# The depthwise convolution of an attention layer: its taps on VectorE, in the second pass of each group of heads

## What is computed

```python
qkvo = einsum('oc,bchw->bohw', qkvo_w, x) + qkvo_b          # q, k, v and a gate o
lepe = conv_general_dilated(v_ch, lepe_w, padding='SAME', feature_group_count=C)   # 5x5, one filter a channel
y    = softmax(q k^T * SCALE) v  + lepe + lepe_b            # 12 heads of 32 channels
x    = x + proj(y * o)
```

## Time and profile before

| what | value |
|---|---|
| median of 3 launches | 11554.08 us (11551.97 to 11557.6) |
| profiled launch, and its span from first to last instruction | 11558.28 us, 11556.5 us |
| TensorE busy | 9370.7 us, 81% |
| VectorE busy | 7579.1 us, 66% |
| ScalarE, GpSimd busy | 4167.8 us, 36%; 3974.5 us, 34% |
| mean granted TensorE clock | 0.84 of full |
| chain that ended last | PE 63%, DVE 20%, ACT 6%, issue 6% |

### The profile page before, as it was taken

How to read it: one execution, slowest core, us unless ns; L and a number is a source line. 1 busy time by engine, 2 the same in 40 slices (tenths; PEclk the granted TensorE clock), 3 DMA queues, 4 the chain that set the end, 5 groups by cost and what they waited for, 6 DMA issues and landing times.

```text
span 11556.5 us, 104310 instructions
## 1 busy us (share of the span) xinstructions
PE 9370.7 (81%) x37272; PEld 4302.3 (37%) x37272; DVE 7579.1 (66%) x5637; ACT 4167.8 (36%) x4762; POOL 3974.5 (34%) x1678
## 2 busy tenths in 40 slices
PE   6985888688986889778896798868898688977656
PEld 2223333443334433344333433344333443334433
DVE  3127666866768566776668666686666866677892
ACT  1114334333333333432344333433334333343441
POOL 0004333432334323443334323343233433343560
PEclk8666888788987989889897898879898798988778
DMA  1002111421114211232113311142111421123231
GB/s 33 4 19 91 48 48 55 128 80 51 50 67 122 71 41 58 86 99 71 48 56 107 92 52 52 57 125 75 52 48 71 119 73 46 50 99 93 85 107 46
DMA packets 423038, 802.30 MB, mean 69 GB/s; under 512 B 226128, under 2 KB 241872, under 8 KB 422352
## 3 DMA queue, kind: packets, MB, share of 16 engines
q1 hardware_dynamic: 422480, 795.13, 21.4%
HBM read 698.28 MB, written 71.04 MB: 67 GB/s over the span
## 4 chain that ended last, share of the span: by engine, by line
PE 63%; DVE 20%; issue 6%; ACT 6%; DMA 2%; DVEq 1%; SPq 1%; ACTq 1%; POOL 0%; POOLq 0%
PE ps L910 10%; DVE R L1654 9%; PE ps L883 8%; PE ps L992 7%; PE ps L863 7%; PE ps L756 7%; PE ps L989 5%; DVE ps L1644 4%; PE ps L894 4%; PE ps L1077 3%; ACT R L1182 3%; PE ps L1060 2%; PE ps L975 2%; DVE nmx L1583 1%; PE ps L965 1%
## 5 line engine op out<-in xcount | busy, mean ns | idle before, releaser
L1368 POOL TENSOR_TENSOR R<-R 128x1024 f32<-128x1024 f32 x1536 | 3678.4, 2396 | 5539.3 <-DVE ps L1644 5512.5
L1654 DVE TENSOR_TENSOR_SCAN R<-R,ps 128x1024 f32<-128x1024 f32 x1536 | 3506.7, 2283 | 537.9 <-ACT R L1242 441.4
L1242 ACT ACTIVATE R<-R,negA 128x1024 f32<-128x1024 f32 x1536 | 1753.8, 1144 | 2773.7 <-DVE R L1654 2515.9
L1644 DVE TENSOR_TENSOR ps<-R 128x1024 f32<-128x1024 f32 x1536 | 1997.1, 1300 | 65.5 <-DVE R L1654 7.0
L992 PEld LDWEIGHTS ps<-ident,R 128*128 128x128 f32 x12288 | 1611.2, 159 | 1115.9 <-issue 789.1
L992 PE MATMUL ps<-ident,R 128*128 128x128 f32 x12288 | 1839.0, 304 | 215.3 <-POOL R L1368 163.5
L1583 DVE TENSOR_REDUCE nmx<-ps 128x2 f32<-128x1024 f32 x768 | 936.2, 1219 | 963.4 <-PE ps L863 958.9
L989 PE MATMUL ps<-R,ident 128*128 128x512 f32 x1440 | 946.1, 792 | 433.9 <-ACT R L1232 430.6
L1182 ACT ACTIVATE R<-ps 128x1024 f32<-128x1024 f32 x768 | 786.1, 1024 | 1324.7 <-PE ps L883 1324.3
L910 PE MATMUL ps<-R 128*128 128x512 f32 x2400 | 1245.0, 642 | 0.0
L883 PE MATMUL ps<-R 33*128 33x512 f32 x3072 | 1017.8, 745 | 160.0 <-ACT R L1182 70.0
(11 more groups left out here) (154 smaller groups left out, 6151.8 us busy)
## 6 DMA issues: line engine op xcount, KB each, us to landing
R<-bc_scratch SPq DMA_DIRECT2D x1024, 512.0 KB, 3.8
R<-in_x SPq DMA_DIRECT2D x72, 512.0 KB, 6.4
out<-R SPq DMA_DIRECT2D x72, 512.0 KB, 2.7
R<-shift_scratch SPq DMA_DIRECT2D x48, 640.0 KB, 10.6
R<-R SPq DMA_DIRECT2D x192, 128.0 KB
R<-out SPq DMA_DIRECT2D x48, 512.0 KB, 7.6
R<-in_w_qkvo SPq DMA_DIRECT2D x32, 576.0 KB, 8.7
rows_scratch<-R SPq DMA_DIRECT2D x24, 512.0 KB, 3.6
```

The source lines that it names most:

```text
L1242: act.activation(decay[i % len(decay)], dt[:, c, :], ACT.Exp, scale=negA[:, col:col + 1]).then_inc(a_sb.h, 1)
L1368: pool.tensor_tensor(state[i % HELD], state[i % HELD], rows_c[slot], ALU.mult).then_inc(hc_sb.h, 1)
L1644: v.tensor_tensor(drive, dtu[:, c, :], rows_b[slot], ALU.mult).then_inc(b_sb.h, 1)
L1654: v.tensor_tensor_scan(h, a, b, 0.0, ALU.mult, ALU.add).then_inc(h_sb.h, 1)
```

## The change

The 25 taps of a group leave TensorE and ScalarE and become 25 VectorE instructions in the second pass. The first is a tensor_scalar that writes `heads`, the others are scalar_tensor_tensor, `heads = window * tap + heads`. Each stands behind a drain, which waits until VectorE's earlier instructions have ended. The first also waits for the first transposed scores of the group, since `heads` shares its place with buffers used before. They are due at even distances over the second pass. The diagonals (`dg`), the copy (`dh`) and their semaphores go.

```diff
--- before.py
+++ after.py
-        for j in range(TAPS):
-            t = at + 1.0 + (S_STEPS - 1.4) * j / TAPS
-            ev += [(t - 1.0, ("dg", g, j)), (t, ("dw", g, j))]
         ev += [(at + (3.0 if g == 0 else 0.3), ("q2", g))]
         at += S_STEPS
-        ev += [(at - 0.1, ("N", g)), (at + 0.5, ("M", g)), (at + 0.55, ("mr", g)), (at, ("dh", g))]
+        ev += [(at - 0.1, ("N", g)), (at + 0.5, ("M", g)), (at + 0.55, ("mr", g))]
         at += N_STEPS
         apart = T_STEPS / TB
+        ev += [(at + 0.15 + (T_STEPS + 0.6) * j / TAPS, ("dw", g, j)) for j in range(TAPS)]
...
                     if kb == 0 and qh == 0:
-                        pe.wait_ge(dh_sb.h, dh_sb.at(img, g + 1))
+                        pe.wait_ge(lv_sb.h, lv_sb.at(img, g + 1))
...
-                if kind == "dw":
-                    m = a
-                    vp = vpad.rearrange("p (h w) -> p h w", w=36)
-                    if j == 0:
-                        pe.wait_ge(lv_sb.h, lv_sb.at(img, m + 1))
-                    pe.wait_ge(dg_sb.h, dg_sb.at(img, TAPS * m + j + 1))
-                    for hf in range(2):
-                        win = vp[:, j // 5 + 16 * hf:j // 5 + 16 * hf + 16, j % 5:j % 5 + WW]
-                        mm = pe.matmul(ps[:, 2 + hf, :], diag[m][j % DIAGS], win, start=j == 0, stop=j == TAPS - 1)
-                    mm.then_inc(dg_ps.h, 1)
...
-                if kind == "dh":
-                    act.wait_ge(dg_ps.h, dg_ps.at(img, TAPS * (a + 1)))
-                    act.activation(heads[:, a, :], banks(2), ACT.Copy).then_inc(dh_sb.h, 1)
-                if kind == "dg":
-                    m = a
-                    if j >= DIAGS:
-                        act.wait_ge(dg_ps.h, dg_ps.at(img, TAPS * m + j - DIAGS + 1))
-                    act.activation(diag[m][j % DIAGS], ident[:, :], ACT.Copy, scale=lepe_w[:, m * TAPS + j:m * TAPS + j + 1])\
-                        .then_inc(dg_sb.h, 1)
...
                     if m:
-                        act.wait_ge(dg_ps.h, dg_ps.at(img, TAPS * m))
+                        act.wait_ge(lp_sb.h, lp_sb.at(img, m))
...
                     v.wait_ge(pv_ps.h, pv_ps.at(img, LB * (a + 1)))
-                    v.wait_ge(dh_sb.h, dh_sb.at(img, g + 1))
...
+                if kind == "dw":
+                    m = a
+                    vp = vpad.rearrange("p (h w) -> p h w", w=36)
+                    sum3 = heads[:, m, :].rearrange("p (h w) -> p h w", w=WW)
+                    win = vp[:, j // 5:j // 5 + HH, j % 5:j % 5 + WW]
+                    tap = lepe_w[:, m * TAPS + j:m * TAPS + j + 1]
+                    v.drain()
+                    if j == 0:
+                        v.wait_ge(lv_sb.h, lv_sb.at(img, m + 1))
+                        v.wait_ge(t_ps.h, t_ps.at(img, TB * m + 1))
+                        v.tensor_scalar(sum3, win, tap, None, ALU.mult)
+                    else:
+                        ins = v.scalar_tensor_tensor(sum3, win, tap, sum3, ALU.mult, ALU.add)
+                    if j == TAPS - 1:
+                        ins.then_inc(lp_sb.h, 1)
```

More of the change, by code:

```diff
@@ L57 @@
 S_STEPS, N_STEPS, T_STEPS = 14, 1.6, 16.2
-TAPS, DIAGS = 25, 8
+TAPS = 25
 def place(i):
@@ L387, in build @@
         vpad = side(14336, 36 * 36)
-        diag = [[side(9216 + K1 * g + P * i, P) for i in range(DIAGS)] for g in range(GROUPS0)]
         rinv = [side(HALF * i, HALF) for i in range(2 * GROUPS0)]
@@ L480, in build @@
         pv_ps = sem("products_done", GROUPS0 * TB // 2)
-        dg_sb = sem("tap_diagonal_ready", TAPS * GROUPS0)
-        dg_ps = sem("tap_summed", TAPS * GROUPS0)
-        dh_sb = sem("depthwise_term_ready", GROUPS0)
+        lp_sb = sem("depthwise_term_ready", GROUPS0)
         o_sb = sem("heads_divided", 2 * GROUPS0)
```

## The result

| | time |
|---|---|
| before | 11553.02 us (median of 4, 11544.88 to 11557.60) |
| after | 12038.88 us (median of 4, 12035.19 to 12052.97) |
| ratio | 1.0424, 95% interval 1.0406 to 1.0442 |
| forecast | 12,350 us, range 11,830 to 12,850, slower 0.89 |

The change makes the kernel 4.2% slower, 486 us. The forecast is 311 us too high, inside its range.

What follows compares the result with a forecast made beforehand. TensorE, busy 81%, was taken as the main bound, with VectorE's chain nearly as long in the first pass. The profiled 11558.3 + 273 + 21 + 6 + 494 gave 12,352, forecast as 12,350 us, range 11,830 to 12,850.

Steps and rivals of the forecast that it cites:

- T beside a scan: Second pass, 21 groups beside a scan: taps' work and waits for GpSimd's port add +23.5 us a group, +494.
- rival A: Second pass: VectorE wins the port from GpSimd, costing only 3 to 5 us a group; 11,940 us, chance 0.20.
- S beside a scan: First pass (scores, row maxima), 21 groups beside a scan: lower TensorE clock costs +13 us a group, +273.
- 9.4 us a step: First pass, all at lower clock: scan step of 7.5 us, plus 1.0 for a third reduce and 0.9 for the reload.
- the 9.0 made of it: First pass: step of 9.0 us at a granted clock near 0.6, a fifth of the time at the upper level.
- the reload of the sum: First pass, once in four scan steps: 3.78 us at the lower clock, charged as 0.9 us a step.
- First image: Three groups without a scan beside them: first pass +7 us each, +21; second pass up to +2 each, +6.
- B: First pass: the clock stays up as in the kernel before; 11,830 us, chance 0.12.
- C: Both passes: TensorE is the bound, so the change makes the kernel faster; 11,335 us, chance 0.07.
- C's second condition: Second pass: the taps meet no GpSimd product; needed for the faster outcome of 11,335 us.
- D: Second pass: TensorE's clock falls to the lower level too; 13,150 us, chance 0.12.
- Two of my signs: Signs expected in the profile: first-pass stretches of 140 to 150 us, and a mean tap near 2.6 us.

Runs made afterwards that it cites:

- filler run: The changed kernel with only the first of 25 taps computed, plus 12 pairs of unread full 128x128 products in each first pass: 11580.84 us.
- the first four experiments: Changed kernel with drains behind taps (11710.32 us), taps behind scans (11700.49), one-input reduces replacing taps 2 to 25 (11678.3), or only the first tap (11656.42).
- one tap: The changed kernel with only the first of each group's 25 taps computed, the other 24 left out: 11656.42 us, ratio 1.0099.

## Why the prediction was right, and where it was not

**T beside a scan: forecast +23.5 a group, measured +18.5, of which 16 is the port.** The mechanism and its price hold: the tap waits 2.14 us (forecast 2.1), the fourth image's stretches grew by 16, 26.4 and 19.3 us (forecast 15, 30, 25). For group 2 the forecast of the stretch itself was right, 139.5 us against 138.4 measured; its growth was too large because I subtracted the 114.0 of a window that stops 5 us early. (The mean of 15, 30 and 25 is 23.3 and not 23.5, which is 4 us of the 494.) Most of the rest of the miss in T is the second image. Forecast and rival A stood 0.01 us apart, and both came true in one run: GpSimd first in images three to eight, VectorE first in the second, whose T grew by 2 to 6 us as A has it (3 to 5). That the race fell to GpSimd in 18 of 21 groups hangs on a margin of 0.01 us, and that part of the hit is luck. In those 18 stretches 246 taps are long, 13.7 a stretch against 14 to 16 forecast. T's part of the 311 is -105 us.

**S beside a scan: forecast +13 a group, measured +3.2. This term was mis-sized; it is -206 of the -311.** The clock came as forecast ("near 0.6": 0.55 to 0.62). The Trainium skill (TensorE: Matmul & The Clock Gate, Part 4: PE-mode transpose), by whose rule S would have been at the lower level nearly throughout and +18, gives a still larger miss. The failed step is "9.4 us a step" and the 9.0 made of it. The second S of the fourth image shows it, cut from the start of one scan to the start of another, before (first two lines) and after (last two):

```profile
4288.63 2.28 DVE L1654 TENSOR_TENSOR_SCAN R<-R,ps 128x1024 f32<-128x1024 f32 x1
...
4384.69 2.28 DVE L1654 TENSOR_TENSOR_SCAN R<-R,ps 128x1024 f32<-128x1024 f32 x1
...
4408.61 2.28 DVE L1643 TENSOR_TENSOR_SCAN R<-R,ps 128x1024 f32<-128x1024 f32 x1
...
4510.87 2.28 DVE L1643 TENSOR_TENSOR_SCAN R<-R,ps 128x1024 f32<-128x1024 f32 x1
```

Both cuts hold 12 steps of the scan and 28 reduces: 96.06 us before and 102.26 after, 8.00 and 8.52 us a step. The step grew by 0.52 and not by the 1.1 between 7.9 and 9.0. (Groups 0 and 2 grew by 4.8 and 5.0 us over the same 12 steps.) Two of the three parts of the sum are right. The plain step with two reduces lasts 7.31 us from scan to scan, or from drive to drive in the timeline above (forecast 7.5), and one with a third reduce 10.71, so 3.40 more as forecast. What was mis-sized is the reload of the sum. I charged it in full, 3.78/4 = 0.9 a step. But eight steps of 7.31 and four of 10.71 make 101.3 us, and the measured 102.26 leave 0.9 us for three reloads, under 0.1 a step. The timeline shows two reasons, the reload beside a reduce and a drive, and the products behind it:

```profile
4470.36 3.67 PE L973 MATMUL ps<-R,ident 128*128 128x512 f32 x4
4470.48 1.23 DVE L1558 TENSOR_REDUCE nmx<-ps 128x2 f32<-128x1024 f32 x1
...
4471.62 1.22 DVE L1633 TENSOR_TENSOR ps<-R 128x1024 f32<-128x1024 f32 x1
...
4474.83 1.13 PE L857 MATMUL ps<-R 32*128 32x512 f32 x4
```

Part of the reload runs while VectorE works, and the score products behind it take 1.13 us in place of 2.08, so they ran at the upper level, and what they save covers most of what the reload takes. Another 3.3 us lie ahead of the cut: from the start of S to the first scan of the cut the kernel after takes 24.8 us and the kernel before 28.1, and the sum held that piece unchanged. 6.2 lost and 3.3 won are the 2.9 us of this group.

The kernel before also had a part that I left out of the sum: its own score products stood in line behind taps on TensorE. Taking those away gave S something, the lower clock took more. The filler run speaks for it, though no run shows it apart: at 0.79, below the 0.89 of before, S is already at 131.1, under the 133.0 of before.

**First image.** S forecast +7 each, measured 114.1 at clock 0.50 against 107.4 in group 1, mean +6.4; T forecast +6 in all, measured -1.3, its taps hidden.

**Other rivals.** B and C wanted the clock up in S; it was not. C's second condition, no collisions, was then made true by placing the taps behind the scan; their work cost 44 us in all, but the kernel stayed 1.4% slower than before, since S gave nothing back. D, T at the lower clock, did not come: 0.78 to 0.85 in the fourth image, and 0.93 again in group 1 with the pace. Two of my signs were off as well: S came out at 134 to 141 us, not 140 to 150, and the mean of the 576 taps at 2.20 us, not 2.6, since no tap of the first and only one of the second image is long.

**Ledger of the 495 us between after and the kernel before as timed beside the first four experiments:** port 338 (after less taps behind the scan), the taps' own work 44 (that less one tap), the rest 113 (one tap less before), of which 99 lie in the first passes at their lower clock. The kernel after was timed beside a kernel before of 11553, so some 10 of the 338 are a difference between batches. What is not settled: why GpSimd comes 0.01 us ahead of the tap in the loop and 0.05 behind it in straight code. No experiment tried it.

## What to carry to other kernels

When work leaves an engine, look at what else it held: here a pair of PSUM banks, worth 760 us once used, against 495 lost by the move itself. A product and the reduce that reads it, in one pair of banks, add up; in two pairs the longer one counts. Beside a scan that was VectorE's work, and TensorE's lower clock hardly mattered; alone in the first image it was the products at the lower clock, 1.90 us a round. Before putting a two-input VectorE instruction near GpSimd work, find the event that releases both, and put the instruction behind another one.

## What the runs showed of the hardware that I had not expected

- One instruction sequence has two outcomes, one in the loop over images and one in straight code: with GpSimd ahead by 0.01 us the tap lasts 3.42 us and the product 2.35, with the tap ahead by 0.05 us 1.28 and 3.45. The first costs some 19 us a stretch, the second about nothing.
- A tensor_scalar over 128x1024 with one tensor in SBUF takes 0.75 us, but 2.9 in four of 24 cases beside a GpSimd product, in three of them though its record starts 0.05 to 0.06 us ahead of the product's.
- Waiting for the port appears as duration of the instruction and not as idle time; a mean (2198 ns for the 576) hides two values, 1286 ns and some 3420. The line with shortest, median and longest shows it.
- Useless full-array products made a kernel faster, by 76 us, as they raised the clock of products that fill 32 rows; alone, such products left the clock at 0.50 to 0.51.
